# Four graph layers and a mixture of experts on one core: expert rows scattered to their picks' places, combining by groups of five tiles, and layer 3's side steps in a new order

## The reference

```python
x  = gc + (feats @ W_res + b_res)              # gc: the aggregated graph convolution
logits = x @ Wg + bg                           # 64 experts
vals, idx = top_k(logits, 2); gates = softmax(vals)
# each row goes to its two experts (at most 1024 rows each): h = gelu(row @ w1 + b1), out = h @ w2 + b2
y  = x + sum over the two picks of gate * out
mean, var over the 3125 rows
layer = (y - mean) * rsqrt(var + 1e-5) * gamma + beta
out = layernorm(feats + layer)
```

## Time and profile before

| | |
|---|---|
| median of three runs | 2125.81 us (2124.03 to 2128.05) |
| the profiled execution | 2125.8 us, span 2124.1 us |
| PE busy | 1819.4 us, 86% |
| PE's weight loads | 1445.4 us, 68% |
| DVE busy | 907.9 us, 43% |
| ACT busy | 466.9 us, 22% |
| POOL busy | 390.2 us, 18% |
| DMA | 553.57 MB, mean 261 GB/s |
| granted PE clock, mean | 0.939 |

### The profile page before, as it was taken

One profiled execution on the slowest core, in us unless ns is written; L12 is line 12 of the kernel. 1 busy time (PEld: TensorE's weight loads), 2 busy tenths in 40 slices (PEclk: granted clock), 3 DMA queues, 4 the chain that ended last, 5 costly groups with the idle time before them and its releaser, 6 DMA issues. The chain is left out here.

```text
span 2124.1 us, 34378 instructions
## 1 busy us (share of the span) xinstructions
PE 1819.4 (86%) x9586; PEld 1445.4 (68%) x9620; DVE 907.9 (43%) x2788; ACT 466.9 (22%) x1245; POOL 390.2 (18%) x723
## 2 busy tenths in 40 slices
PE   1988885999899899999989999899993999999451
PEld 0355554788688788777778878688882888888220
DVE  4976664444434411122211157736665121222256
ACT  0034444322222211111111111111110332232010
POOL 1022223311111200000000012214443111111451
PEclk8999997999999999999999999999996999999656
DMA  4178999999588688766668889889973999999421
GB/s 123 31 249 305 324 324 348 315 321 326 183 294 264 201 271 288 260 216 215 215 214 289 289 275 289 266 269 307 309 250 131 327 372 369 359 373 371 160 71 60
DMA packets 284900, 553.57 MB, mean 261 GB/s; under 512 B 17170, under 2 KB 208328, under 8 KB 281608
## 3 DMA queue, kind: packets, MB, share of 16 engines
q1 hardware_dynamic: 275976, 528.36, 75.1%
q0 software_dynamic: 8832, 24.13, 3.3%
HBM read 415.14 MB, written 137.29 MB: 260 GB/s over the span
## 5 line engine op out<-in xcount | busy, mean ns | idle before, releaser
L1001 PE MATMUL psum<-xsa,blk 128*128 128x512 f32 x2500 | 639.3, 405 | 18.1 <-DVEq L356 8.2
L1001 PEld LDWEIGHTS psum<-xsa,blk 128*128 128x128 f32 x2500 | 462.4, 191 | 106.5 <-issue 10.7
L1001 PE MATMUL psum<-xsb,blk 128*128 128x512 f32 (+1 forms) x1875 | 416.2, 369 | 6.0 <-DVEq L356 5.9
L1001 PEld LDWEIGHTS psum<-xsb,blk 128*128 128x128 f32 x1875 | 321.6, 190 | 64.8 <-issue 7.0
L1360 DVE TENSOR_SCALAR onehots<-counts_scratch 128x348 bf16<-128x348 f16 x464 | 161.6, 374 | 79.9 <-issue 41.5
L903 PE MATMUL psum<-onehots 128*128 128x349 bf16 x464 | 146.7, 316 | 40.8 <-DVE onehots L1365 38.5
L509 PE MATMUL psum<-route,expert_weights 128*128 128x128 f32 x1360 | 169.0, 278 | 0.0
L1759 POOL TENSOR_SCALAR ve<-mv 128x1 f32<-128x1 f32 x75 | 16.8, 223 | 820.5 <-DVE mv L1475 820.5
L906 PE MATMUL psum<-zrow 128*128 128x512 bf16 x431 | 160.8, 381 | 0.0
L509 PEld LDWEIGHTS psum<-route,expert_weights 128*128 128x128 f32 x1360 | 159.8, 193 | 0.9
L519 PE MATMUL psum<-expert_weights,route 128*128 128x256 f32 x672 | 159.1, 380 | 0.6 <-ACT route L568 0.6
(11 more groups left out here) (299 smaller groups left out, 2076.8 us busy)
## 6 DMA issues: line engine op xcount, KB each, us to landing
blk<-counts_src_on_rows SPq DMA_DIRECT2D x125, 832.0 KB, 4.7
blk<-counts_src_on_rows SPq DMA_DIRECT2D x125, 768.0 KB
expert_weights<-in_L_gnn_w SPq DMA_DIRECT2D x176, 512.0 KB, 6.1
blk<-counts_dst_on_rows SPq DMA_DIRECT2D x50, 832.0 KB, 4.5
counts_dst_on_rows<-band_rows SPq DMA_DIRECT2D x25, 1600.0 KB, 8.4
blk<-counts_dst_on_rows SPq DMA_DIRECT2D x50, 768.0 KB
counts_src_on_rows<-blk SPq DMA_DIRECT2D x13, 1600.0 KB, 8.6
counts_src_on_rows<-rblk SPq DMA_DIRECT2D x12, 1600.0 KB, 9.7
```

The source lines that it names most:

```text
L1001: mm = e.matmul(o, blk[n][:, k * P:(k + 1) * P], XS[:, k, :, 0:Fw], start=(k == 0), stop=(k == T - 1 and not own))
```

## The change

It changes five things.

1. **Scattered results.** Next to each row, layer 3 also scatters the number of its pick, four bytes, to `pick_of_row` in DRAM. SP writes numbers of spare places there during the loading, loads all of them back as one tile when every scatter has landed, PE transposes them and DVE keeps them as integers. In the experts' loop POOL copies the chunk's column of them and stores the chunk's rows by an indirect DMA at their picks' places, so that the two results of a node lie side by side. `expert_rows_out` is cleared over 22 x 384 KB instead of 22 x 768 KB.
2. **Combining by five tiles.** SP loads five tiles' pairs of rows with one plain DMA (five in all), ACT multiplies them by their gates, DVE adds pair to pair and to x4 over 1280 elements, and sums the five tiles into one (`tensor_reduce` over a view in which the tile is the innermost dimension), so that PE's matmul with ones is made once per group. The squares go the same way. The last tile's spare rows are cleared by a factor instead of a masked matmul.
3. **Adding beta to X** moves from DVE, in combining, to POOL, ahead of the experts' loop.
4. **The last stage.** ACT applies the final scale and shift; POOL makes the shift with two more small instructions per group.
5. **Layer 3's order.** Each side step is done as early as its inputs allow, two turns deep instead of five, and the barriers "l3" and "route" are gone: semaphores carry their dependences.

```diff
@@ sync_moe
-            phase_end(e, "l3")
-            e.wait_ge(S("rows_zeroed"), 2 * 16 * (T - 3))
-            carry_wait(e)
             e.wait_ge(S("experts_known"), 1)
-            phase_end(e, "route")
+            e.wait_ge(S("rows_scattered"), 2 * 16 * TOP * T)
+            e.dma_start(pick_rows[0:NCH, :], ids[0:NCH * P, :].rearrange("(c p) a -> c (p a)", p=P)).then_inc(S("inputs_loaded"), 16)
             for c in range(RING):
                 load_rows(c, c)
...
             phase_end(e, "experts")
+            for g in range(T // SPLIT):
+
+                lo, hi = g * SPLIT, (g + 1) * SPLIT
+                e.dma_start(picked_rows[:, lo:hi, :, :].rearrange("p t k f -> p t (k f)"),
+                            ybuf[TOP * lo * P:TOP * hi * P, :].rearrange("(t p k) f -> p t (k f)", t=SPLIT, p=P))\
+                    .then_inc(S(f"outs_in{g}"), 16)
+            for g in range(T // SPLIT):
+                e.wait_ge(S(f"outs_in{g}"), 16)
             phase_end(e, "combine")
@@ pe_moe
+            e.wait_ge(S("inputs_loaded"), 16 * (LOADS + 2))
+            e.transpose(psum[:, 6, 0:P], pick_rows[:, :], identF[:, :]).then_inc(S("ids_turned"), 1)
             turn(0, 0, 0, 0)
...
+            for n, (name, buf) in enumerate((("combined", sums_of), ("squares_added", squares_of))):
+                for g in range(T // SPLIT):
+                    e.wait_ge(S(name), g + 1)
+                    mm = e.matmul(psum[:, n, 0:F], ones[:, :], buf[:, g, :], start=(g == 0), stop=(g == T // SPLIT - 1))
+                mm.then_inc(S("bn_summed"), 1)
@@ act_moe
+            for t in range(T):
+                if t % SPLIT == 0:
+                    e.wait_ge(S(f"outs_in{t // SPLIT}"), 16)
+                for k in range(TOP):
+                    v = picked_rows[:, t, k, :]
+                    e.activation(v, v, ACT.Copy, scale=gate[:, k, t:t + 1]).then_inc(S("picks_scaled"), 1)
+            for g in range(T // SPLIT):
+                lo, hi = g * SPLIT, (g + 1) * SPLIT
+                e.wait_ge(S("centred"), g + 1)
+                if hi == T:
+
+                    hi -= 1
+                    e.activation(picked_rows[:, hi, 1, :], X4[:, hi, :], ACT.Square, scale=valid[:, hi:hi + 1])\
+                        .then_inc(S("squared"), 1)
+                e.activation(picked_rows[:, lo:hi, 1, :], X4[:, lo:hi, :], ACT.Square).then_inc(S("squared"), 1)
             phase_end(e, "combine")
+            for g in range(T // SPLIT):
+                e.wait_ge(S("out_shift"), g + 1)
+                for t in range(g * SPLIT, (g + 1) * SPLIT):
+                    e.activation(X4[:, t, :], X4[:, t, :], ACT.Identity, scale=out_r[:, t:t + 1], bias=out_shift[:, t:t + 1])\
+                        .then_inc(S("out_made"), 1)
@@ dve_moe
+            e.wait_ge(S("ids_turned"), 1)
+            e.tensor_copy(pick_of[:, :], psum[:, 6, 0:P]).then_inc(S("picks_known"), 1)
...
+            def over_tiles(v):
+                return v.rearrange("p t f -> p f t")
+
+            for g, b in enumerate(groups):
+                e.wait_ge(S("picks_scaled"), TOP * SPLIT * (g + 1))
+                y0, y1 = picked_rows[:, b, 0, :], picked_rows[:, b, 1, :]
+                st.done(e.tensor_tensor(y0, y0, y1, ALU.add))
+                st.done(e.tensor_tensor(X4[:, b, :], X4[:, b, :], y0, ALU.add))
+                e.tensor_reduce(sums_of[:, g, :], over_tiles(X4[:, b, :]), AX.X, ALU.add).then_inc(S("combined"), 1)
...
+            def add_squares(g):
+                e.wait_ge(S("squared"), g + 1 + (g == len(groups) - 1))
+                e.tensor_reduce(squares_of[:, g, :], over_tiles(picked_rows[:, groups[g], 1, :]), AX.X, ALU.add)\
+                    .then_inc(S("squares_added"), 1)
+
+            for g, b in enumerate(groups):
+                e.tensor_tensor(X4[:, b, :], X4[:, b, :], G[:, :].unsqueeze(1).to_broadcast([P, SPLIT, F]), ALU.subtract)\
+                    .then_inc(S("centred"), 1)
+                if g:
+                    add_squares(g - 1)
+            e.wait_ge(S("centred"), len(groups))
+            add_squares(len(groups) - 1)
@@ pool_moe
+            for g in range(T // SPLIT):
+
+                b = slice(g * SPLIT, (g + 1) * SPLIT)
+                e.tensor_tensor(X[:, b, :], X[:, b, :], bc["bet"][:, :].unsqueeze(1).to_broadcast([P, SPLIT, F]), ALU.add)
+            e.wait_ge(S("picks_known"), 1)
...
+                    e.wait_ge(S(f"rows_stored{n}"), 16 * j)
+                    carry_wait(e)
+                    e.tensor_copy(pick_col[n][:, :], pick_of[:, bass.ds(c, 1)]).then_inc(S("pick_taken"), 1)
+                    e.wait_ge(S("pick_taken"), c + 1)
                     e.wait_ge(S("chunk_made"), c + 3)
-                    e.dma_start(ybuf[bass.ds(c * P, P), :], yout[n]).then_inc(S(f"rows_stored{n}"), 16)
+                    carry_wait(e)
+                    e.indirect_dma_start(out=ybuf, out_offset=bass.IndirectOffsetOnAxis(ap=pick_col[n][:, 0:1], axis=0),
+                                         in_=yout[n], in_offset=None).then_inc(S(f"rows_stored{n}"), 16)
@@ layer 3 on PE, DVE and POOL
             aggregate("l3", XSa, F, False, [
                 (1, own_turned),
+                (2, ranks),
                 (1, turn("l3", "sum_read", "g_turned", pT, G, KF)),
-                (4, ranks),
-                (2, turn("l3", "x4_made", "x4_turned", px4, V, KF)),
                 (1, dense("l3", ["xT", "gT"], "pre", pD[0], two(tT, wgc) + two(tT2, wrs))),
-                (2, dense("l3", ["x4T"], "logits", pD2[0][:, 0:NE], two(tT3, wgt)))])
+                (1, turn("l3", "x4_made", "x4_turned", px4, V, KF)),
+                (1, dense("l3", ["x4T"], "logits", pD2[0][:, 0:NE], two(tT3, wgt)))])
...
-            pipeline(e, [(1, l3_sum), (2, l3_x4), (3, l3_top), (4, l3_slots)], unrolled=True)
-            dve_moe(e)
+            pipeline(e, [(2, l3_top), (1, l3_sum), (2, l3_slots), (1, l3_x4)], unrolled=True)
+            dve_moe(e, st)
...
+                    e.indirect_dma_start(out=ids, out_offset=bass.IndirectOffsetOnAxis(ap=slot_to[:, k, i:i + 1], axis=0),
+                                         in_=pick_id[:, k, i:i + 1], in_offset=None).then_inc(S("rows_scattered"), 16)
...
-            pipeline(e, [(2, l3_keep), (5, l3_scatter), (4, l3_pages)], unrolled=True)
+            pipeline(e, [(2, l3_pages), (1, l3_keep), (2, l3_scatter)], unrolled=True)
```

More of the change, by code:

```diff
@@ L30 @@
 FALL = 65536.0
+LOADS = 32
 PAGE_STEPS = 7
@@ L95, in gnn_program @@
     xbuf = nc.dram_tensor("expert_rows_in", (TRASH + TOP * NP, F), F32, kind="Internal").ap()
-    ybuf = nc.dram_tensor("expert_rows_out", (YCH * P, F), F32, kind="Internal").ap()
+    ybuf = nc.dram_tensor("expert_rows_out", (TOP * NP + NCH * P, F), F32, kind="Internal").ap()
+    ids = nc.dram_tensor("pick_of_row", (TRASH + TOP * NP, 1), F32, kind="Internal").ap()
     with ExitStack() as ctx:
@@ L176, in gnn_program @@
         slot_to = sb("slot_to", [P, TOP, T], U32)
-        slot_from = sb("slot_from", [P, TOP, T], U32)
+        pick_id = sb("pick_id", [P, TOP, T])
+        pick_rows = sb("pick_rows", [P, P])
+        pick_of = sb("pick_of", [P, P], U32)
+        pick_col = [sb(f"pick_col{n}", [P, 1], U32) for n in range(RING)]
         def view(buf, at, n, dt):
@@ L290, in gnn_program @@
         assert at <= 10240
-        w1s, w2s, xin, xTs, hTs, yout, b2s, ring = ([] for _ in range(8))
+        w1s, w2s, xin, xTs, hTs, yout, b2s = ([] for _ in range(7))
         for base, lot, room in ((mw, ((w1s, (KF, H), RING), (w2s, (HT, F), RING)), T * PARTS * F * 2),
@@ L301, in gnn_program @@
             assert at <= room
[L302 to L311, removed]
+        picked_rows = mw[:, :].bitcast(F32).rearrange("p (t k f) -> p t k f", t=T, k=TOP)
+        at = 0
+        sums_of, at = cut(mx, at, (T // SPLIT, F))
+        squares_of, at = cut(mx, at, (T // SPLIT, F))
+        out_stats, at = cut(mx, at, (T, 6))
+        out_mv, at = cut(mx, at, (T, 2))
+        out_r, at = cut(mx, at, (T,))
+        out_shift, at = cut(mx, at, (T,))
+        bn_r, at = cut(mx, at, (KF,))
+        assert at <= 10240
         psum = ctx.enter_context(nc.psum_tensor("psum", [P, 8, BANK], F32))
@@ L322, in gnn_program @@
         block = ctx.enter_context(nc.Block())
-        PHASES = ["load", "table", "l0", "l1", "h1a", "h1b", "h2a", "h2b", "l3", "route", "experts",
+        PHASES = ["load", "table", "l0", "l1", "h1a", "h1b", "h2a", "h2b", "experts",
                   "combine"]
@@ L647, in dve_moe @@
-            e.wait_ge(S("combined"), T)
+            st.done(e.tensor_scalar(X4[:, T - 1, :], X4[:, T - 1, :], valid[:, T - 1:T], None, ALU.mult))
+            groups = [slice(g * SPLIT, (g + 1) * SPLIT) for g in range(T // SPLIT)]
+            def over_tiles(v):
[6 more added lines that the diff above has]
+                e.tensor_reduce(sums_of[:, g, :], over_tiles(X4[:, b, :]), AX.X, ALU.add).then_inc(S("combined"), 1)
@@ L701, in pool_moe @@
             phase_end(e, "experts")
```

(12 more changed lines are left out.)

125 lines of the change are left out of this document (50 added, 75 removed).

## The result

The changed kernel takes 2104.04 us, the median of four runs (2101.84 to 2108.33), against 2126.39 (2124.03 to 2128.05): a ratio of 0.989 (0.988 to 0.991), 22.4 us less.

The account below looks back on a forecast made before the run. It took PE to bound layer 3, DMA the experts, neither the combining, and DVE the last stage; +8.2 - 15.2 + 0.7 - 20.4 - 4.0 = -30.7 from 2125.8 gave 2095.1, told as 2095.0 us, range 2070 to 2117.

Parts of the forecast that it names:

- The change leaves all up to 1380.56 alone: Everything ahead of layer 3 keeps its time, apart from one small DMA and two iotas under the loading: 0 us.
- Layer 3, +8.2: Layer 3: PE waits 0.29 us per tile for x4, 23 times, +6.7; side steps inside the aggregation add 1.5.
- Last own rows to first expert rows, -15.2: From layer 3's last own-row transposes to the first expert rows: 26.4 us against 41.6, with scatters landing in 2.0.
- Rival B: Ring 0.9 a tile (+14), scatter priced as gather (+8.7), or landing as long as the barrier's (+2.2): 2097 to 2120; chance 0.17.
- Experts, +0.7: Experts' stage, bound by DMA: 84 scatters instead of plain stores at 0.009 us more each; chunks still 3.9 us apart.
- Combining, -20.4: Combining: plain loads and sums over five tiles replace gathers, 41.8 + 10R = 75.8 us against 96.2.
- R: One DVE sum over five tiles in combining, ten in all: taken as 3.4 us, ends 1.45 and 6.95.
- rival A: Combining's sums run at the plain rate, R 1.45, and layer 3 has no ring wait: about 2069, with the wait 2076; chance 0.2.
- Last stage, -4.0: Last stage: five scalings a group leave DVE for ACT, so 29.8 us to the last scaling against 33.8.
- the +3 that was feared: Last stage: POOL, held up beside DVE's wide additions, falls a group behind, +3 us.
- C: Rival, combining: DVE's ten reductions cost more than the gathers they replace, slower from R = 6.5; 2130.5 at 6.95; chance 0.09.
- D: Rival, layer 3: four-byte scatters take POOL far over 1.26 us; at 2.7, 31 us more, level with before; chance 0.04.

Follow-up runs that it names:

- e1: The kernel before plus an unused tile of 1152 bytes a partition ahead of the aggregation's operands: 2144.62 us, ratio 1.009.
- e2: The changed kernel with its new tiles placed so that every other tile lies where it did in the kernel before: 2090.13 us, ratio 0.982.
- e5: The changed kernel with DVE making x4 before the slots of its turn instead of after them: 2153.66 us, ratio 1.013.
- e9: e10 with layer 3 reordered: DVE does aggregated sum, choice, x4, slots; PE's ranks stand behind the pre-activation: 2079.63 us, ratio 0.978.
- e8: The changed kernel storing the experts' rows by plain DMAs, without the column copy (output means nothing): 2104.22 us.
- e10: The changed kernel with e2's operand places and PE summing tile by tile instead of DVE's ten reductions: 2076.97 us, ratio 0.976.

## Why the prediction was right, and where it was not

The sign and the range were right and 2095 was 9 us off, but by errors that cancel: +17.7 and +8.0 against -12.4, -5.9 and -1.2, together +6.2 on -30.7.

- **"The change leaves all up to 1380.56 alone"** is the step that failed outright. It looked at instructions and not at what the new tiles do to the addresses behind them. 13.2 us of the 17.7 are that (e1, e2); 4.5 are the clock while the counts are made, seen in executions of both programs.
- **Layer 3, +8.2:** measured +7.0. The tile of 9.06 came as 9.03, with PE's weight load waiting 0.43 for x4. The closeness is in part luck: the forecast's own steps, x4 ready at 6.28 and wanted at 6.05, give a wait of 0.23 and not 0.29, and its slots leave out 0.09 us of the last instruction's 0.29. e5 and e9 confirm that DVE's order sets the tile.
- **Last own rows to first expert rows, -15.2:** measured -7.2. The plain rows' landing of 2.0 was used for the four-byte scatters too; rows land in 1.5 and other tiles' four bytes in as little as 1.2, but the last tile's in 6.4, outside the ends 2.0 to 4.2. Another 2.4 us: the last scatter starts 23.3 us behind the own rows and not 20.9, with PE's last pre-activation, transposes and logits at the lower level of the granted clock (0.50 from 1626.50 to 1634.00). And PE waits first for the pick ids, asked for 0.4 us ahead of the rows and there 3.2 us later. Rival B had the landing, at less than its size, and put it down to the barrier.
- **Experts, +0.7:** measured -5.2. The chunks are 3.85 apart at 370 GB/s, where "still 3.9" was forecast; over 84 chunks the 0.06 is the 5 us. Pricing scatter as store was right (e8); the gain is not explained.
- **Combining, -20.4:** measured -32.8. The mechanism and the count were right, one term was mis-sized: R is 2.33 and not 3.4, ten times, 10.7 us. The way from the squares' sum to the last stage took 4.6 and not 6.35, mainly because DVE is idle for 0.15 us behind the barrier where it was for 2.52. The first group came at 10.7 and not 9.5: the loads' 385 GB/s doesn't follow from its row, 4.19 MB at 77.6% of 16 us, which gives 338, and the first load's data were there after 6.6 us and not 5.5. R lies between rival A's 1.45 and the forecast. Steps of 1 KB (L671, 2332 ns) and of 2 KB (L678, 2329 ns) cost the same. At the 4.3 ns a result of the earlier trace rows 256 results alone give 2.55, so the second addition, the step's 0.66 ns an element, was one too many; the two can't be told apart here. By the Trainium skill's rule (SBUF — State Buffer, Door 1: The DMA port swizzle) the step costs something over 1.45; the 0.88 more agree in sign, but the results alone could make them up.
- **Last stage, -4.0:** measured -4.0, 30.1 us from the barrier to the last scaling. POOL's power is 2.40 beside DVE's additions and the first of its small steps 1.39 (0.24 alone), but POOL still keeps up, with 0.46 us to spare in a group of 5.0, so the +3 that was feared by the Trainium skill's rule (SBUF — State Buffer, Who interferes with whom) didn't come.
- Rivals C and D fell: R is far from 6.5, and PE is busy for 224.65 of layer 3's 224.80 us, with a four-byte scatter issued in 0.97.

## What to carry to other kernels

A tile that is added or taken away moves every tile behind it. Where a matmul streams from one of those all through the span, compare the addresses before and after and the median duration of the untouched matmuls, and put the new tile last, or keep the move to a distance that costs nothing (256 and 1024 bytes here): that was worth more than half of what the whole change gained. Price a scatter's landing by where its rows go, spare rows too, and not by another scatter's; when a wait in a ring is taken out, look at which other step of the same engine stands between two things the bottleneck waits for.

## What was not expected of the hardware

- Operands moved by 1152 bytes a partition: 393 ns a matmul for 389, 15.7 us over six aggregations; by 256 or 1024: nothing.
- 128 four-byte writes of an indirect DMA, 75 of them to neighbouring words, land 6.4 us behind the issue, where an ordinary tile's land in as little as 1.2 and 128 rows of 1 KB in 1.5; loads asked for meanwhile came after 7.0 us, at a DMA share of 1.45 and 36 GB/s.
- More matmuls, kept dense, ran at more than twice the pace: in combining PE's granted clock was 0.50 with 22 matmul records and 0.75 with 102 (e10), and a matmul of 256 fp32 columns took 0.24 us a pass where it took 0.61. The kernel before had 104 records there, spread out, and 0.57.
